# Three edits to an eight-stage decoder kernel: loads moved into the first stage, norms and output of the state space re-timed, local layers entered group by group

## The chip, the cores and the metric

The kernel runs on one core of a Trainium2 chip, as one program. The metric is the device time of the whole program in microseconds (us). Engines are named as the profile names them: PE (TensorE), DVE (VectorE), ACT (ScalarE), POOL (GpSimd) and SP (SyncE, which only issues DMAs here). All arithmetic is in float32, apart from one split into bf16 parts in the state space.

## The reference

A residual stream x of 16 sequences, 256 positions and 128 channels passes eight stages, each fed by a LayerNorm without gain or bias.

```python
x = x + causal_linear_attention(ln(x))   # "favor": 16 heads of 64, 128 random features
x = x + router_ffn(ln(x))                # "router"
x = x + cosine_attention(ln(x))          # "cosine"
x = x + int4_linear(ln(x))               # "int4"
x = x + state_space(ln(x))               # "mamba": inner 256, 16 states, silu gate
x = x + expert_ffn(ln(x))                # "experts": 8 experts, top 2
x = x + gated_recurrence(ln(x))          # "hgrn"
y = ln(x)                                # "local": 6 layers on y
for i in range(6):
    y = y + local_attention(shift_tokens(y), window=32) @ Wo[i]
    y = y + (a * gelu(gate)) @ W2[i] + b2[i]   # a, gate from an affine LayerNorm of the shifted y
return x + y
```

`shift_tokens` delays the upper half of the channels by one position. In the state space, for each of 256 inner channels and 16 states, h = exp(delta·A)·h + delta·x·B runs along the sequence, and C reads it out.

## The kernel before

**Tiles and groups.** x stays in SBUF as 32 tiles of 128 positions. Four tiles make a group of 512 columns (`GT` = 4, `GROUPS` = 8). Each stage is written as one loop of steps, and in a step each engine has its own list of helper calls, in an order set by hand. Engines meet only at semaphores: an instruction list is run in order, so a wait holds back all that stands behind it on its engine. Between blocks (`nc.Block()`) all engines meet.

**First block** (`build`, L2852 to L2866). SP issues group 0 of x, nine constants, the favor weights, the rest of x, and then 38 loads for the stages router, cosine, int4, mamba and hgrn (`Weights.load`, L2744). Then it waits for the constants. The other engines have nothing to do in it.

**First stage** (`favor_attention`). 64 pairs of heads, one a step; step i projects pair i. In a step SP runs `send_inverse(i - 5)`, 4 DMAs, and `send_norm(i - 1)`, 8 DMAs, which spread small rows over the partitions. DVE's `lower(n)` waits for the norms of pair n, `normalize(n)` for its inverse. At step 0, DVE's list begins with `measure(1)`, the statistics of group 1, and it waits there for x's second load; the copy of the first projection (`take`, L423) stands behind it.

**State space** (`state_space`). A step k is one state of one group: 16 steps a group, 128 in all. DVE: `drive_with(k)` (L1432), then other work that is due, then `scans(k)` (L1442). PE: `spread_rows(k)` (L1247 and L1250), `gather(k - 2)` (L1258), then work that is due. `drive_with(k)` needs `spread_rows(k)`, and that the drive before it is done. Work of the next group and of the last one is due at fixed places of the 16:

```python
MEASURE, NORMALIZE, TURN, TURNED, WIDEN, LOWER, BIAS, LOWER_C, BIAS_C, LAST_DT, SPLIT_ALL, SOFTPLUS, DELTA = \
    0, 1, 2, 3, 5, 7, 8, 9, 10, 11, 12, 13, 14
GATE, WAY_OUT, ADD_OUT = 2, 3, 4
```

The first gather of a group (at place 2) waits until DVE has read the sums of the group before (`skip_and_gate`, place 2). `project_out` (24 products) is all at place 3 on PE. `widen` (place 5) alternates with ACT's `silu`, and its second product waits for `add_out` of two groups before, since both use bank 1.

**Local layers** (`local_layers`). A block of its own comes first: SP issues 8 constants, 2 rows of scales and 11 weights; DVE takes statistics of all 32 tiles (L2190, L2193), then normalizes group after group (L2202), PE turns each group (L2230), and ACT and DVE copy the two halves into y (L2223, L2207). DVE then takes the peaks of the scales. The main block has 32 steps a layer, four quads of heads for each group, and step i runs four projections `project(4i)` to `project(4i + 3)`. Each goes round a ring: PE projects into the one bank (L2254), DVE multiplies it twice (`rotate_start`, L2539 and L2540), ACT squares it (`square`, L2433), and PE's next projection waits for that square. POOL sums squares and multiplies by the inverse norms (L2645, L2653), which come by 4 DMAs a step. PE's output projection of a group is in two parts at step 4G + 6. At a layer's start DVE makes eight tables ahead of its first rotation (`scale_tables`, L2527 and L2528). Bank 7 (`X_BANK`) is used in turns; `take_x` waits until the user before has been read.

## Time and profile before

| | |
|---|---|
| time, median of 3 runs | 6522.08 us (6519.73 to 6525.92) |
| time of the profiled execution | 6522.74 us |
| its span | 6520.8 us |
| busy: PE, DVE, ACT, POOL | 90%, 67%, 52%, 35% |
| mean granted PE clock | 0.947 |
| first stage | 38 to about 900 us |
| scan of the state space | 1819 to about 2475 us |
| local layers, with the block ahead | 3201 to 6520 us |

A timeline row gives start, duration, engine, line, operation, names and count, and in brackets how long the engine had been idle and what ended that. SPq rows are DMA issues on SP. A window row gives the stretch and its length, then the busy time and count of PE, PEld, DVE, ACT and POOL, the granted clock of PE (1.00 is 2.4 GHz, 0.50 is 1.2 GHz) and the load of the DMA engines.

### The profile page before, as it was taken

Reading aid. Unit: us, or ns where it says so; the run is one execution under the profiler, and the core shown is the slowest. Engines: PE = TensorE matmul, PEld = TensorE weight load, DVE = VectorE, ACT = ScalarE, POOL = GpSimd, SP = SyncE. Lnnn points to the kernel's source line nnn. Section 1 sums busy time; section 2 is a strip of 40 time slices with the busy share of each in tenths; the row PEclk is TensorE's granted clock in tenths of the full one; section 3 lists DMA queues with packets and bytes.
Section 4 is the critical chain, followed back from the end, with each engine's and each line's share of the span. In section 5 each row is a group of like instructions: output and inputs, shape, how many; then the busy total and the mean of one; then the engine's idle time right before and its main releaser. Section 6 shows DMA issues by size and latency. Waiting matters only on the chain.

```text
span 6520.8 us, 129965 instructions
## 1 busy us (share of the span) xinstructions
PE 5878.9 (90%) x51681; PEld 3219.8 (49%) x51681; DVE 4384.8 (67%) x7178; ACT 3402.6 (52%) x5560; POOL 2289.2 (35%) x1597
## 2 busy tenths in 40 slices
PE   7999878999677778998689999999999999999998
PEld 3555554444422225765445555555555555555554
DVE  4656434454288894334678888888878788887885
ACT  3444324656144443444456656666666666665664
POOL 0111101222034441000055555555555555555553
PEclk9999978999688888998799999999999999999998
DMA  5555302333100000000011111111111111111110
GB/s 138 115 115 119 89 0 53 80 82 83 44 3 0 0 0 1 1 0 1 24 36 32 40 43 34 31 47 37 34 45 38 33 44 40 34 39 41 38 37 24
DMA packets 298945, 275.95 MB, mean 42 GB/s; under 512 B 40580, under 2 KB 289572, under 8 KB 298148
## 3 DMA queue, kind: packets, MB, share of 16 engines
q1 hardware_dynamic: 298372, 268.00, 17.7%
q8 instruction: 397, 6.50, 0.4%
q14 instruction: 176, 1.44, 0.1%
HBM read 30.88 MB, written 2.10 MB: 5 GB/s over the span
## 4 chain that ended last, share of the span: by engine, by line
PE 33%; issue 5%; DVE 5%; POOL 5%; ACT 2%; DMA 0%; POOLq 0%; DVEq 0%; SPq 0%; ACTq 0%
PE banks L2254 7%; PE banks L2289 6%; PE banks L2324 5%; PE banks L2309 4%; PE banks L2267 3%; PE banks L2341 3%; DVE local_probs L2559 2%; POOL local_rot L2653 2%; POOL local_ssum L2645 2%; PE banks L2363 2%; PE banks L2313 2%; PE banks L2274 1%; ACT local_probs L2455 1%; DVE local_gate L2584 1%; DVE local_sin L2540 1%
## 5 line engine op out<-in xcount | busy, mean ns | idle before, releaser
L2645 POOL TENSOR_TENSOR local_ssum<-local_sq 128x512 f32<-128x512 f32 x384 | 697.5, 1816 | 2145.1 <-ACT local_sq L2433 2144.6
L2653 POOL TENSOR_TENSOR local_rot<-local_rot,local_inv_all 128x512 f32<-128x512 f32 x768 | 964.6, 1288 | 94.1 <-DMA local_inv_all<-local_inv 93.6
L2254 PE MATMUL banks<-local_y,local_Wqkv 128*128 128x512 f32 x1536 | 823.0, 618 | 64.0 <-ACT local_sq L2433 61.2
L2559 DVE TENSOR_TENSOR local_probs<-banks,band 128x576 f32<-128x576 f32 x768 | 546.2, 753 | 185.4 <-PE banks L2289 180.1
L2455 ACT ACTIVATE local_probs<-local_probs,local_npeak 128x1152 f32<-128x1152 f32 x384 | 482.8, 1257 | 357.1 <-DVE local_probs L2559 357.1
L2539 DVE TENSOR_TENSOR local_rot<-banks,local_rotary_scaled 128x512 f32<-128x512 f32 x768 | 525.6, 684 | 191.1 <-PE banks L2254 185.6
L2433 ACT ACTIVATE local_sq<-banks 128x512 f32<-128x512 f32 x768 | 459.4, 598 | 253.6 <-DVE local_sin L2540 244.8
L2546 DVE TENSOR_TENSOR local_rot<-local_rot,local_sin 128x1024 f32<-128x1024 f32 x384 | 513.7, 1338 | 41.9 <-DVE local_sin L2540 2.3
L2449 ACT COPY local_v<-banks 128x512 f32<-128x512 f32 x384 | 224.9, 586 | 594.1 <-PE banks L2267 593.6
L2289 PEld LDWEIGHTS banks<-local_rot 32*128 32x128 f32 x12288 | 416.7, 186 | 225.0 <-issue 200.8
L2540 DVE TENSOR_TENSOR local_sin<-banks,local_rotary_scaled 128x512 f32<-128x512 f32 x768 | 522.4, 680 | 0.0
L2309 PEld LDWEIGHTS banks<-local_probs,local_v 128*32 128x32 f32 x12288 | 345.4, 110 | 301.8 <-issue 291.9
L2289 PE MATMUL banks<-local_rot 32*128 32x160 f32 (+1 forms) x12288 | 490.2, 296 | 0.0
L1361 POOL TENSOR_TENSOR mamba_seen<-mamba_state,mamba_c_wide 128x1024 f32<-128x1024 f32 x128 | 301.0, 2352 | 474.2 <-DVE mamba_state L1442 474.2
L2309 PE MATMUL banks<-local_probs,local_v 128*32 128x160 f32 (+1 forms) x12288 | 458.5, 290 | 0.5 <-DVE local_oT L2567 0.5
L2254 PEld LDWEIGHTS banks<-local_y,local_Wqkv 128*128 128x128 f32 x1536 | 264.3, 190 | 372.1 <-ACT local_sq L2433 249.5
L1031 POOL TENSOR_TENSOR cosine_summed<-cosine_probs 128x512 f32<-128x512 f32 x128 | 162.4, 1269 | 696.1 <-ACT cosine_probs L919 696.1
L2267 PE MATMUL banks<-local_Wqkv,local_y 128*128 128x512 f32 x768 | 396.0, 597 | 0.0
L2324 PE MATMUL banks<-local_oT,local_Wo 128*128 128x512 f32 x768 | 354.9, 605 | 0.9 <-ACT local_gate L2477 0.9
L1258 PE MATMUL banks<-mamba_seen,ident 128*128 128x512 f32 x512 | 289.2, 693 | 64.8 <-DVE mamba_xs L1449 42.3
L2341 PE MATMUL banks<-local_mlp_z,local_W 128*128 128x512 f32 (+1 forms) x576 | 328.2, 652 | 11.9 <-DVE local_gate L2584 4.2
L487 POOL TENSOR_TENSOR favor_summed<-favor_probs 128x256 f32<-128x256 f32 x128 | 93.0, 727 | 689.3 <-DVE favor_probs L443 689.3
(400 smaller groups left out, 10561.4 us busy)
## 6 DMA issues: line engine op xcount, KB each, us to landing
local_inv_all<-local_inv SPq DMA_DIRECT2D x768, 128.0 KB, 2.7
favor_half_norm_all<-favor_half_norm SPq DMA_DIRECT2D x512, 128.0 KB, 3.0
cosine_inv_all<-cosine_inv SPq DMA_DIRECT2D x256, 128.0 KB, 2.6
favor_rden<-favor_inv SPq DMA_DIRECT2D x256, 64.0 KB, 2.1
cosine_rden<-cosine_inv_den SPq DMA_DIRECT2D x256, 64.0 KB, 2.1
local_Wqkv<-in_L_ffn_Wqkv_quads SPq DMA_DIRECT2D x36, 256.0 KB, 2.9
local_Wo<-in_L_ffn_Wo_quads SPq DMA_DIRECT2D x6, 512.0 KB, 4.1
experts_w_W<-in_L_ffn_W SPq DMA_DIRECT2D x1, 2048.0 KB
```

Of the source, the lines that this page charges most:

```text
L2254: pe.matmul(seqs(banks[:, QK_BANK, :]), Wqkv[:, at:at + P], y_group(g), start=True, stop=True).then_inc(qk_projected, 1)
L2267: pe.matmul(banks[:, V_BANK, :], y[:, 2 * g + tile // ST, at:at + P], Wqkv[:, V_COLUMNS(half)], start=True, stop=True).then_inc(v_projecte ...
L2289: last = pe.matmul(banks[:, S_BANK + r, lo:hi], k[rows_r, half, at:at + P], q[rows_r, half, at:at + hi - lo], start=(half == 0), stop=(hal ...
L2309: last = pe.matmul(banks[rows_r, O_BANK, part * SEQ + at:part * SEQ + to], v[:, G % 2, s * ST + tile, c:c + 32], probs[:, e % 3, r, lo:hi] ...
L2324: last = pe.matmul(banks[:, X_BANK, :], Wo[:, j, :], oT[:, (QUADS * G + j // 2) % (QUADS + 1), j % 2, :], start=(j == 0), stop=(j == 2 * Q ...
L2341: pe.matmul(banks[0:m, X_BANK, :], W1[:, column + lo:column + lo + m], z[:], start=True, stop=True).then_inc(signal, 1)
L2455: act.activation(a, a, ACT.Exp, bias=npeak[:, layer:layer + 1], scale=SCALE).then_inc(exped, 1)
L2539: dve.tensor_tensor(seqs(rot[:, k % ROTATED, half, :]), raw, twice(table[:, m, 0, half, :]), ALU.mult).then_inc(cosined, 1)
L2540: dve.tensor_tensor(seqs(sin[:, m, half, :]), raw, twice(table[:, m, 1, half, :]), ALU.mult).then_inc(sined, 1)
L2559: dve.tensor_tensor(probs[:, e % 3, r:r + 2, :], banks[:, S_BANK + r:S_BANK + r + 2, 0:SCORES], consts["band"].unsqueeze(1).broadcast_to([ ...
L2645: pool.tensor_tensor(ssum[:, n % 2, m, :], sq[:, 0, :], sq[:, 1, :], ALU.add).then_inc(square_summed, 1)
L2653: pool.tensor_tensor(a, a, twice(inv_all[:, n % 2, m, of_seq(s)]), ALU.mult).then_inc(united, 1)
```

## The change

**One, loads.** The first block keeps group 0 of x, four constants, the favor weights and the rest of x. The other five constants are issued by SP within the first stage, at step 1, and the loads of router, cosine, int4, mamba and hgrn at steps 2 to 6, each time behind that step's `send_norm`. The order among the loads is kept. At the end of its list for the stage SP waits for all constants.

**Two, state space.** The norm of the next group is due four places earlier (places −4 to −1, that is 12 to 15 of the group before), the loop starts four steps earlier, PE's turn waits in addition until bank 0 is free, `project_out` is halved over places 3 and 4, and `add_out` is at place 5.

**Three, local layers.** The block ahead norms, turns and copies group 0 alone; ACT now copies both halves. Group i + 1 is measured, rooted and normalized in step i, and turned and copied in step i + 1, for i = 0 to 6, through bank 7 and a tile of 512 columns. The four tables of q are made at the end of the step before a layer starts, the four of k behind the first rotation.

```diff
# favor_attention, SP
+                    if i == LOADS:
+                        for tile, source in w["later_consts"]:
+                            sp.dma_start(tile, source).then_inc(w["consts_loaded"][0], 16)
+                    if 0 < i - LOADS <= len(w["later"]):
+                        w["later"][i - LOADS - 1].load(sp)
+                sp.wait_ge(*w["consts_loaded"])
...
# state_space
-        0, 1, 2, 3, 5, 7, 8, 9, 10, 11, 12, 13, 14
-    GATE, WAY_OUT, ADD_OUT = 2, 3, 4
-    FIRST, LAST = -NS, N + ADD_OUT
+        -4, -3, -2, -1, 5, 7, 8, 9, 10, 11, 12, 13, 14
+    GATE, WAY_OUT, ADD_OUT = 2, (3, 4), 5
+    FIRST, LAST = MEASURE - NS, N + ADD_OUT
...
                 def turn(m):
                     pe.wait_ge(normed, GT * (m + 1))
+                    if m:
+                        pe.wait_ge(dt_biased, CH * m)
...
-                def project_out(g):
+                def project_out(g, half):
                     pe.wait_ge(gated, CH * (g + 1))
-                    for t in range(GT):
+                    for t in range(half * GT // 2, (half + 1) * GT // 2):
...
-                    if (g := finish_at(k, WAY_OUT)) is not None:
-                        project_out(g)
+                    for half in range(2):
+                        if (g := finish_at(k, WAY_OUT[half])) is not None:
+                            project_out(g, half)
...
# local_layers, helpers of the entry
+        def measure(dve, g):
+            for tile in tiles_of(g):
+                dve.bn_stats(ln_stats[:, tile, :], x[:, tile, :]).then_inc(stats_done, 1)
+            for tile in tiles_of(g):
+                dve.wait_ge(stats_done, tile + 1)
+                dve.bn_aggr(ln_moments[:, tile, :], ln_stats[:, tile, :]).then_inc(moments_done, 1)
...
+        def normalize_x(dve, g):
+            dve.wait_ge(rstd_ready, g + 1)
+            if g:
+                dve.wait_ge(turned, g)
...
+        def turn_x(pe, g):
+            pe.wait_ge(normed, GT * (g + 1))
+            for tile in range(GT):
+                last = pe.transpose(banks[:, X_BANK, tile * P:(tile + 1) * P], xn[:, tile, :], consts["ident"])
+            last.then_inc(turned, 1)
+
+        def copy_x(act, g):
+            act.wait_ge(turned, g + 1)
+            for side, a in y_sides(g):
+                act.copy(a, seqs(banks[side, X_BANK, :])).then_inc(y_ready, 1)
...
# PE, in project(c), and in a step behind score(odd)
+                        if layer == 0 and quad == 0:
+                            pe.wait_ge(y_ready, 2 * (g + 1))
...
+                    if 1 <= i < GROUPS:
+                        take_x(y_ready, 2 * (i + 1))
+                        turn_x(pe, i)
...
# ACT, behind exp(odd) and ahead of square(4i + 3)
+                    if 1 <= i < GROUPS:
+                        copy_x(act, i)
+                    if i < GROUPS - 1:
+                        root_x(act, i + 1)
...
# DVE
                     if i < N:
+                        if i == 0:
+                            scale_tables(0, 0)
+                        rotate_start(4 * i)
                         if i % STEPS == 0:
-                            scale_tables(i // STEPS)
-                        rotate_start(4 * i)
+                            scale_tables(i // STEPS, 1)
...
                         rotate_start(4 * i + 1)
                         rotate_end(2 * i)
+                        if i % STEPS == STEPS - 1 and i < N - 1:
+                            scale_tables(i // STEPS + 1, 0)
+                    if i < GROUPS - 1:
+                        measure(dve, i + 1)
...
                         rotate_start(4 * i + 3)
                         rotate_end(2 * i + 1)
+                    if i < GROUPS - 1:
+                        normalize_x(dve, i + 1)
...
# build
+FAVOR_CONSTS = ("ident", "ones", "heads_of_pair", "causal")
-                for n in consts:
+                for n in FAVOR_CONSTS:
                     sp.dma_start(consts[n], t[n]).then_inc(consts_loaded, 16)
                 ws["favor"].load(sp)
                 sp.dma_start(x[:, GT:TILES, :], rows[:, GT:TILES, :]).then_inc(x_rest, 16)
-                for name in ("router", "cosine", "int4", "mamba", "hgrn"):
-                    ws[name].load(sp)
-                sp.wait_ge(consts_loaded, 16 * len(consts))
+                sp.wait_ge(consts_loaded, 16 * len(FAVOR_CONSTS))
```

## Rows read from the trace of the kernel before

**Rows 1.** Timeline, first 60 us: start, duration, engine, line, operation, count [idle before].
```profile
9.12 1.14 SPq L2860 DMA_DIRECT2D x<-in_L_attn_x  x1
10.30 8.39 SPq L2744 DMA_DIRECT2D router_w_W1T<-in_L_ffn_W1T  x1
...
37.42 0.43 SPq L2744 DMA_DIRECT2D hgrn_w_norm_w<-in_L_attn_norm_w  x1
...
45.38 0.69 DVE L423 COPY favor_qk<-banks 128x512 f32<-128x512 f32 x1 [2.76 <-PE banks L240]
```

**Rows 2.** DMA issues: count, KB each (misread where uneven), median us to landing.
```profile
local_rot<-in_L_ffn_k_scale SPq DMA_DIRECT2D x1, 192.0 KB, 5.6
...
x<-in_L_attn_x SPq DMA_DIRECT2D x1, 0.5 KB, 13.3
```

**Rows 3.** Timeline of SP's queue alone in the first stage, steps 1 to 6.
```profile
55.34 28.42 SPq L194 DMA_DIRECT2D favor_half_norm_all<-favor_half_norm  x32
87.86 2.48 SPq L205 DMA_DIRECT2D favor_rden<-favor_inv  x4
90.45 5.22 SPq L194 DMA_DIRECT2D favor_half_norm_all<-favor_half_norm  x8
98.36 2.47 SPq L205 DMA_DIRECT2D favor_rden<-favor_inv  x4
```

**Rows 4.** Timeline of the state space, second group's last steps and the join behind.
```profile
1903.17 2.10 DVE L1382 TENSOR_SCALAR mamba_xn<-x,mamba_moments,mamba_rstd 128x128 f32<-128x128 f32 x4
...
1910.23 3.60 PE L1258 MATMUL banks<-mamba_seen,ident 128*128 128x512 f32 x4 [6.31 <-DVE mamba_xs L1449]
...
1914.60 1.23 DVE L1432 TENSOR_TENSOR banks<-mamba_dx,banks 128x1024 f32<-128x1024 f32 x1 [1.07 <-PE banks L1247]
...
1915.86 2.33 DVE L1442 TENSOR_TENSOR_SCAN mamba_state<-mamba_decay,banks 128x512 f32<-128x512 f32 x2
1916.26 0.61 PE L1266 MATMUL banks<-mamba_w_Wout,mamba_xs 128*128 128x128 f32 x4
...
1920.88 1.23 DVE L1432 TENSOR_TENSOR banks<-mamba_dx,banks 128x1024 f32<-128x1024 f32 x1 [2.68 <-PE banks L1247]
...
1924.69 1.88 PE L1212 MATMUL banks<-mamba_xnT,mamba_w_Win 128*128 128x512 f32 x4
1924.97 1.23 DVE L1432 TENSOR_TENSOR banks<-mamba_dx,banks 128x1024 f32<-128x1024 f32 x1
...
1930.14 1.23 DVE L1432 TENSOR_TENSOR banks<-mamba_dx,banks 128x1024 f32<-128x1024 f32 x1 [1.57 <-PE banks L1247]
```

**Rows 5.** Timeline of the entry to the local layers.
```profile
3201.52 6.29 DVE L2190 BATCH_NORM_STATS2 local_mlp_z<-x 128x6 f32<-128x128 f32 x32 [4.53 <-PEq L46]
...
3206.68 0.55 SPq L2176 DMA_DIRECT2D local_rot<-in_L_ffn_k_scale  x1
...
3213.79 0.37 SPq L2160 DMA_DIRECT2D local_W<-in_L_ffn_W  x1
...
3232.06 1.11 DVE L2202 TENSOR_SCALAR local_rot<-x,local_mlp_sq,local_mlp_yc 128x128 f32<-128x128 f32 x4
...
3236.59 2.04 PE L2254 MATMUL banks<-local_y,local_Wqkv 128*128 128x512 f32 x2 [2.24 <-PEq L2168]
```

**Rows 6.** Windows (PE, PEld, DVE, ACT, POOL busy, PEclk, DMA) of layer steps; timeline.
```profile
3236.60:3254.60 18.00, 11.67 (x12) 3.31 (x12) 9.10 (x18) 3.36 (x6) 1.75 (x1) 0.50 0.00 0
...
3285.80:3299.50 13.70, 12.34 (x180) 7.01 (x181) 11.85 (x18) 8.35 (x15) 7.72 (x6) 1.00 0.19 41
...
3297.66 1.26 ACT L2455 ACTIVATE local_probs<-local_probs,local_npeak 128x1152 f32<-128x1152 f32 x1 [1.40 <-DVE local_probs L2559]
...
3344.23 0.69 DVE L2539 TENSOR_TENSOR local_rot<-banks,local_rotary_scaled 128x512 f32<-128x512 f32 x1 [3.04 <-PE banks L2254]
```

**Rows 7.** Timeline of VectorE where the second layer starts.
```profile
3767.05 0.34 DVE L2527 TENSOR_SCALAR local_rotary_scaled<-local_rotary,local_qk_scales 128x256 f32<-128x256 f32 x1
...
3776.78 1.53 DVE L2592 SCALAR_TENSOR_TENSOR local_y<-banks,local_b,local_y 64x512 f32<-64x512 f32 x2 [0.92 <-PE banks L2363]
```

More of the change, by code:

```diff
@@ L142, in favor_attention @@
     OUTS = 11
+    LOADS = 1
     A_BANK, F_BANK, S_BANK, O_BANK, DEN_BANK, X_BANK = 0, 1, 3, 5, 6, 7
@@ L2188, in _ @@
             def _(dve):
[L2189 to L2195 removed]
+                measure(dve, 0)
                 dve.memset(up_half[:], 16.0 * float(np.log(2.0))).then_inc(started, 1)
@@ L2199, in _ @@
                 dve.memset(y[high, :, 0:1], 0.0).then_inc(started, 1)
[L2200 to L2207 removed]
+                normalize_x(dve, 0)
                 dve.wait_ge(rows_in, 32)
@@ L2216, in _ @@
                 act.preload_act_table_set(EXP_LN)
[L2217 to L2223 removed]
+                root_x(act, 0)
+                copy_x(act, 0)
             @block.tensor
             def _(pe):
[L2227 to L2231 removed]
+                turn_x(pe, 0)
         with nc.Block() as block:
@@ L2534, in rotate_start @@
                     k = 2 * n + m
+                    if n % STEPS == 0 and half == 0:
+                        dve.wait_ge(tabled, 8 * layer_of(n) + 4 * m + 4)
                     dve.wait_ge(qk_projected, c + 1)
```

81 lines of the change are left out of this document (38 added, 43 removed).

## Prediction

> **What bounds the kernel now.** I read the page first. TensorE is busy for most of the span, but that is an average over eight stages, so each edit is priced in its own stage, from the timeline: which wait ends last there. Four places matter.
>
> The start: no engine works on data before the first block ends, and that block ends when SP has issued its last load, at 37.85 us [rows 1]. Most of these loads are not wanted before hundreds of us later.
>
> The first stage in its steady state repeats every 10.5 us, and SP issues 2.48 us of DMAs for the inverse and 5.22 us for the norms in it [rows 3]: 7.7 us of 10.5, so SP has 2.8 us to spare per step.
>
> The state space: a step of VectorE is the drive, 1.23 us, and two scans, 2.33 together, 3.63 with the gaps between them; at the join of two groups it also waits for TensorE's row spreads (L1247) [rows 4]. These waits are all that a reordering there can win.
>
> The entry of the local layers: TensorE's first projection starts at 3236.59, and the block ahead of it is VectorE's walk over all 32 tiles from 3201.52 on; SP's last issue there is over at 3214.16 [rows 5]. In the steps behind it VectorE is busy for 11.85 of 13.7 us [rows 6], so work put there is not free.
>
> **Part one, the loads.** Five constants leave the first block: 0.43 us for an issue like the last one in the rows and 0.05 to the next, 2.4 us [rows 1]. All loads from `router_w_W1T` to `hgrn_w_norm_w` leave too: from 10.30 to 37.85, 27.55 us. The block would end at 7.9. But VectorE comes to `measure(1)` before the first copy of a projection, and that waits for the rest of x. Its load was issued 1.18 us before `W1T`, at 9.12, and took 13.3 us to land [rows 2]: 22.4, in the new order 2.4 us earlier, 20.0. `measure(1)` is four tiles of statistics at 0.2 us [rows 5] and by my estimate 0.6 of aggregations and sum: 1.4. The copy behind it started at 45.38, because it waited for TensorE, which it won't by then. So the copy starts at 20.0 + 1.4 + 0.1 = 21.5 in place of 45.38: **23.9 us won**, and not the 30 us by which the block is shorter. The favor weights are issued ahead of x's rest and hide behind it, as does the first projection.
>
> The price is paid in the first stage's steps 1 to 6. The moved issues cost SP 27.55 less the 7.96 us by which `W1T`'s own 8.39 exceeds its neighbours' 0.43 [rows 1], 19.6 for 38 loads, and 2.4 for the constants: 22.0 us. On SP they stand behind `send_norm` and in front of the next step's `send_inverse` and `send_norm`; VectorE's `lower` and `normalize` wait for those. From 55.34, SP would have six norms (31.3), two inverses (5.0) and the loads (22.0) to issue before the third inverse: free at 113.6 where it is wanted at 87.86 + 21 = 108.86 [rows 3]. That is **4.8 us late, which I take as lost**. Low end 2 (a norm that lands ahead of its use absorbs the rest). A gain is excluded, since nothing is taken off SP there. High end: each of the five groups of loads stalls as `W1T` did, 8 us apiece, 45 us; what made `W1T` slow, 1.8 MB of x just issued, has an equal only in the cosine group, so 13 is my practical high end. The new wait for the constants at the end of SP's program ends long before. Net of part one: 19.1.
>
> **Part two, the state space.** VectorE's work per group is the same wherever the norm stands, so only TensorE's order counts. At the join of two groups: the gather after the skip connection starts at 1910.23 and takes 3.6 us, the next spread comes behind the four transposes, and VectorE idles 1.07 until 1914.60; then the whole projection out, from 1916.26, makes it idle 2.68 until 1920.88; widening starts at 1924.69 and makes it idle 1.57 more [rows 4]. Between the gather's end and VectorE's start lie 0.8 us, by my estimate half of it the transposes: without them the first wait is 0.6. Between 1916.26 and 1920.88 lie 4.6 us, 0.5 of it the spread up to VectorE's start, so the projection is 4.1. With halves of 2.05 us each, TensorE needs 0.5 (spreads, to VectorE's start) + 1.6 (gather, 1914.60 to 1916.26) + 2.05 = 4.15 a step against VectorE's 3.63: two waits of 0.5 in place of 2.68. The third step gets no `add_out`, so it takes 4.15 as against 4.09 before. But TensorE now comes to the widening without its lead: 1.7 us after VectorE's step start, where it was 0.28 us before it, so that step grows by 1.95 us. Sum from 1913.53 to 1930.14: before 16.6, after 0.6 + 4.15 + 4.15 + 7.1 = 16.0: 0.6 us for a group. If the gather runs at the upper clock (1.7 us in place of 3.6, since VectorE reaches the skip 1.9 us sooner, the norm of 2.10 having moved) TensorE regains its lead and it is 2.0. Seven joins: 4 to 14 us. I take **5**, near the low end, because nothing in the rows shows the clock kept over a gap of 4.4 us. The low bound below that is −4, if the longer way to the widening also delays ScalarE's next decays at every join. The extra steps ahead of the first hold no work of their own.
>
> **Part three, the local layers.** The block ahead now holds one group: norm, four transposes and copies are over by 3209. The peaks wait for the `k_scale` load, 3206.68 + 5.6 [rows 2, 5], plus the 1.2 us of reduction: 3213.5. SP's last issue ends at 3214.16 and sets the end; the first projection starts at 3214.5 in place of 3236.59: **22.1 won**.
>
> The other seven groups now run inside steps 0 to 7. On VectorE each costs `measure`, 0.2 us a tile for the statistics [rows 5] and, with aggregations and sum, 1.4 as in part one, and a normalization, 1.11 with GpSimd idle [rows 5] or 2.10 with it busy [rows 4]; GpSimd works in most of these steps, so 3.5 together for the pair at most and 2.5 at least. On ScalarE: two copies and two roots, by my estimate 1.6, put between `exp` and the `square` that releases the next projection. In steps 2 to 5 `exp` (3297.66 + 1.26) ends just when `square` is due [rows 6], so these 1.6 and VectorE's normalization are both late, side by side: 1.7. `measure` costs 1.4 less the 0.5 of VectorE's wait for the scores: 0.9. So 2.6 a step, 10.4 for four. Step 0 has wide waits because TensorE runs at the low clock there: 0.6. Step 1: 1.9. In step 6 VectorE waits 3.04 us for TensorE's output projection [rows 6], which hides its part; ScalarE's and the transposes' leave about 0.5 each in steps 6 and 7. **14 us paid**, 8.1 net.
>
> Here the Trainium skill speaks against the change: SBUF — State Buffer, section "Who interferes with whom", says that VectorE's scalar-tensor operations can take a port pair that they share with GpSimd, whole and for the full instruction. By that rule the seven normalizations cost 2.1 each, by the rows of the idle prologue 1.11; the payment would be 16 or 12. The row beside a busy GpSimd (2.10) agrees with the rule.
>
> The tables at a layer's start are eight operations of 0.26 us apart, all ahead of the first rotation [rows 7]. Split four and four they free that rotation by 1.05 us; VectorE has no gap there until 3776.78, where it waits 0.92 for TensorE [rows 7]. Between 0 and 0.9 at each of five layers: **1.5**.
>
> **Sum**: 19.1 + 5 + 8.1 + 1.5 = 33.7. The profiled execution took 6522.7 (its span is 6520.8), 0.7 above the median: 6522.1 − 33.7 = 6488, say **6489**.
>
> **The rivals.**
> - SP becomes the first stage's bound: every group of loads stalls its queue. For it: SP is at 73% there and `W1T` once took 8.39 us. Against: the groups are a step apart. 13 to 45 us in place of 4.8: 6497 to 6529, most likely 6505.
> - The new work in the layers is hidden. For it: the chain of waits in steps 1 to 6 runs through GpSimd and the transfer of the norms rather than VectorE. Paid 3 in place of 14: 6478.
> - It adds up instead, VectorE's 3.5, ScalarE's 1.6 and TensorE's 0.5 in series, 5 us in seven steps: 35 paid, 6510.
> - The change doesn't do what it says at the joins: TensorE is late for the widening in any order, no gain in part two: 6494.
> - Slower: TensorE's clock. Step 0 runs at a granted 0.5, the lower level of 1.2 GHz, and takes 18.0 us; step 3 at 1.00 (2.4 GHz) takes 13.7 [rows 6]: 4.3 us a step. If the waits that the by-group work puts into the first steps keep TensorE at the lower level, they give back the whole gain and the 13 us beside it after 11 steps; with 16, 6489 + 69 = 6558. Against: the level rose within two steps, in spite of wide gaps.
>
> **How the numbers follow.** Forecast 0.50 (6481 to 6497), SP bound 0.12, hidden 0.16, in series 0.11, no gain at the joins 0.07, clock 0.04. The range 6474 to 6505 takes in the hidden case and the bounds of parts one and two, and leaves out most of the series case, the clock and SP's upper half. 0.2% is 13 us, about what a measurement of this kernel can tell from no change. Only the clock ends beyond it: slower 0.04; half of SP's and of the series case end within it: same 0.10; faster 0.86.
>
> **What would show it.** First copy of `favor_qk` near 21.5; the spacing of `favor_rden`'s issues above 10.5 us for three or four steps, then back; at a join of the state space VectorE's waits for the row spreads near 0.6, 0.5 and 0.5, and a longer one in the widening step; the first layer projection 22 us after the first layer load less 9, that is 13 us after it in place of 35; steps 2 to 5 of the layers at 16 to 17 us. The prediction is wrong if x's rest lands much later than 20, or if steps 1 to 7 grow by over 5 us each.

## The result, and the profile after

| | before | after |
|---|---|---|
| median of the timed runs | 6522.08 us (6519.73 to 6533.43, 5 runs) | 6484.81 us (6481.32 to 6486.44, 5 runs) |
| ratio to before, 95% interval | | 0.9943 [0.9933, 0.9954] |
| profiled execution, its span | 6520.8 us | 6482.8 us |
| mean granted clock | 0.947 | 0.950 |

The forecast was 6489. Timed again beside e9 (below), the changed kernel had 6476.88 us and a ratio of 0.9926 [0.9913, 0.9940]. The two intervals overlap, and the kernel's own median moved by 8 us between them: a few microseconds can't be read from medians, so the parts are followed in the traces, by the start of the same instruction in each.

The ledger of the two profiled executions, in us that the changed kernel is ahead of the one before. It comes from starts of VectorE's instructions. (In the kernel before the last `favor_oT` starts at 798.0 us and the stage is over at 811, not near 900.)

```
first copy of favor_qk                 25.3   (20.06 against 45.38)
end of the first stage (last favor_oT) 17.6
state-space stage, first statistics    17.3
first drive of the scan                15.2
last drive of the scan                 26.1
local block, first rotation            48.9
local layers, head of step 9           34.8
last rotation of the last layer        37.3
span                                   38.0
```

**The start.** VectorE's timeline. The columns are start, duration, engine, line, operation, tiles, count and [idle before and what ended it].

```profile
18.80 0.87 DVE L409 BATCH_NORM_STATS2 favor_stats<-x 128x6 f32<-128x128 f32 x4 [7.38 <-DMA x<-in_L_attn_x]
...
20.06 0.69 DVE L430 COPY favor_qk<-banks 128x512 f32<-128x512 f32 x1
```

The first row ends its wait with the landing of x's rest, issued at 6.87 and so 11.9 us on its way; the copy answers to the one at 45.38 [rows 1].

**SP's queue in the first stage** (the send of the inverses, L206), with one group of loads in front of the third, and VectorE's two waits for what they carry:

```profile
65.94 2.49 SPq L206 DMA_DIRECT2D favor_rden<-favor_inv  x4
...
80.33 2.49 SPq L206 DMA_DIRECT2D favor_rden<-favor_inv  x4
...
88.13 0.61 SPq L2786 DMA_DIRECT2D hgrn_w_Wq<-in_L_attn_Wq  x1
...
92.58 3.67 SPq L206 DMA_DIRECT2D favor_rden<-favor_inv  x4
...
101.73 2.48 SPq L206 DMA_DIRECT2D favor_rden<-favor_inv  x4
...
84.35 0.69 DVE L457 TENSOR_TENSOR favor_oT<-banks,favor_rden 128x512 f32<-128x512 f32 x1 [2.76 <-DMA favor_rden<-favor_inv]
...
97.79 0.69 DVE L457 TENSOR_TENSOR favor_oT<-banks,favor_rden 128x512 f32<-128x512 f32 x1 [3.86 <-DMA favor_rden<-favor_inv]
```

Before, these sends were 10.5 us apart [rows 3]. Here the distances are 14.4, 12.3 and 9.2, and VectorE stands 2.76 and 3.86 us.

**The join of two state-space groups**, the same one as in [rows 4]: VectorE's drives with their waits.

```profile
1895.77 1.23 DVE L1442 TENSOR_TENSOR banks<-mamba_dx,banks 128x1024 f32<-128x1024 f32 x1 [0.99 <-PE banks L1256]
...
1900.23 1.23 DVE L1442 TENSOR_TENSOR banks<-mamba_dx,banks 128x1024 f32<-128x1024 f32 x1 [0.87 <-PE banks L1256]
...
1904.40 1.23 DVE L1442 TENSOR_TENSOR banks<-mamba_dx,banks 128x1024 f32<-128x1024 f32 x1 [0.57 <-PE banks L1256]
...
1911.51 1.23 DVE L1442 TENSOR_TENSOR banks<-mamba_dx,banks 128x1024 f32<-128x1024 f32 x1 [3.05 <-PE banks L1256]
```

The waits were 1.07, 2.68, none and 1.57 before; they are 0.99, 0.87, 0.57 and 3.05. Their sum is no smaller: 5.3 before, 5.5 after.

**The entry of the layers.** TensorE's first projection (before at 3236.59 [rows 5]), then step 6: TensorE's output projection, ScalarE's exponential and copy ahead of it, and VectorE's first rotation of the next step.

```profile
3187.76 2.04 PE L2280 MATMUL banks<-local_y,local_Wqkv 128*128 128x512 f32 x2 [9.45 <-PEq L2214]
...
3300.91 1.25 ACT L2484 ACTIVATE local_probs<-local_probs,local_npeak 128x1152 f32<-128x1152 f32 x1 [0.73 <-DVE local_probs L2592]
3302.07 1.17 ACT L2212 COPY local_y<-banks 64x512 f32<-64x512 f32 x2
...
3303.34 6.61 PE L2350 MATMUL banks<-local_oT,local_Wo 128*128 128x512 f32 x8 [3.72 <-issue]
...
3310.84 0.69 DVE L2572 TENSOR_TENSOR local_rot<-banks,local_rotary_scaled 128x512 f32<-128x512 f32 x1 [9.97 <-PE banks L2280]
```

The copy L2212 is what empties bank 7, and the projection out takes this bank: it starts 0.1 us behind the copy's end, after 3.72 us of idleness, and its eight products take 6.61 us. VectorE stands 9.97 us, where it stood 3.04 before in this place [rows 6].

Windows of step 0 and step 3 (columns: window, length, busy us of PE, PEld, DVE, ACT and POOL, granted clock, DMA share, GB/s); before, they were 18.0 and 13.7 us long [rows 6]:

```profile
3187.70:3205.00 17.30, 10.87 (x13) 3.49 (x14) 10.63 (x27) 3.66 (x8) 2.06 (x2) 0.60 0.24 70
3239.00:3256.00 17.00, 14.34 (x187) 8.11 (x188) 15.97 (x30) 10.58 (x20) 9.19 (x7) 1.00 0.15 32
```

Step 3 has VectorE busy for 15.97 of 17.0 us, where it was busy for 11.85 of 13.7, and TensorE's clock is 1.00 in both: VectorE's 4.1 us of added work are enough for the 3.3 by which it is longer.

### The profile page after: what moved, and what is told of

It reads as the page before. It is cut to its first block, busy times and chain, and to the rows that moved or that the text cites. A ratio compares the mean times of both kernels' runs of the same rounds, so it can differ in the third digit from the quotient of the medians.

```text
span 6482.8 us, 130017 instructions
## 1 busy us (share of the span) xinstructions
PE 5881.0 (91%) x51681; PEld 3217.2 (50%) x51681; DVE 4381.4 (68%) x7177; ACT 3410.3 (53%) x5582; POOL 2283.7 (35%) x1597
## 3 DMA queue, kind: packets, MB, share of 16 engines
q1 hardware_dynamic: 298372, 268.00, 17.8%
## 4 chain that ended last, share of the span: by engine, by line
PE 31%; issue 8%; POOL 7%; DVE 3%; ACT 2%; POOLq 0%; DMA 0%; SPq 0%; DVEq 0%; ACTq 0%
PE banks L2280 7%; PE banks L2315 5%; PE banks L2350 4%; PE banks L2335 4%; POOL local_rot L2694 4%; PE banks L2293 3%; POOL local_ssum L2686 3%; PE banks L2367 3%; PE banks L2389 2%; PE banks L2339 2%; DVE local_probs L2592 2%; PE banks L2300 1%; ACT local_probs L2484 1%; ACT local_sq L2462 0%; PE banks L2363 0%
## 5 line engine op out<-in xcount | busy, mean ns | idle before, releaser
L2686 POOL TENSOR_TENSOR local_ssum<-local_sq 128x512 f32<-128x512 f32 x384 | 683.1, 1779 | 2137.0 <-ACT local_sq L2462 2136.6
L2579 DVE TENSOR_TENSOR local_rot<-local_rot,local_sin 128x1024 f32<-128x1024 f32 x384 | 499.7, 1301 | 40.8 <-DVE local_sin L2573 0.9
L2367 PE MATMUL banks<-local_mlp_z,local_W 128*128 128x512 f32 (+1 forms) x576 | 329.1, 654 | 19.6 <-DVE local_gate L2617 11.9
```

The costliest lines, as they stand in the source:

```text
L2367: pe.matmul(banks[0:m, X_BANK, :], W1[:, column + lo:column + lo + m], z[:], start=True, stop=True).then_inc(signal, 1)
L2686: pool.tensor_tensor(ssum[:, n % 2, m, :], sq[:, 0, :], sq[:, 1, :], ALU.add).then_inc(square_summed, 1)
```

## The experiments

Each kernel is compared with the kernel before by its time, and by its trace with whatever it stands beside.

### One part alone: e1, e2, e3

e1 has only part one's edits of the diff above, e2 only part two's, e3 only part three's.

> The kernel before with part one alone: only the loads needed by the first stage are issued at entry, those of the later stages within its steps. Theory (the parts act apart and add up; the changed kernel's trace has the first stage's last product 17.6 us earlier, and 17.3 at the state-space stage's start): 17.5 us shorter, about 6504.5, with the first x copy near 20 and the sends of favor_rden at spacings of about 14.4, 12.3, 9.2, 10.5 us. Rival (the later stages and the start of the local layers depended on the order of loads, so part of the gain seen in the whole belongs to the other parts or is eaten at a later stage's first load): 10 us or less, over 6512.

> The kernel before with part two alone: in the state-space stage the norm of the next group moved to before the seam of two groups, and the output product in two halves. Theory A (the work taken off the seams is all of it, the gain seen over that stage in the whole kernel, 10.3 us, is its own): about 6511.8, with the scan's period per group lower in the groups whose gather after the seam runs at the upper clock. Theory B (the forecast's sum of 5 us was right for the part itself and the rest of the 10.3 is a drift of the clock that came with the changed start): about 6517.

> The kernel before with part three alone: the local layers entered by groups and their tables split. Theory A (entry gains 21.1 us, the layers' first eight steps give back 14.1 and the rest wins about 3, as the whole kernel's trace shows): 10 us shorter, about 6512, with the stall of TensorE ahead of project_out at step 6 near 3.7 us and that step near 26.8 us. Theory B (the loss at step 6 is chance in the phase of the first steps and comes from the shifted start): step 6 back at about 20.3 us, and 16 us shorter, about 6506.

| | median, us | ratio to before | span | lead at the first stage's end | won in the state space | won at the entry | won in layer steps 0 to 8 | lead at the last rotation |
|---|---|---|---|---|---|---|---|---|
| before | 6519.16 | | 6520.8 | | | | | |
| e1 | 6498.56 | 0.9967 [0.9955, 0.9979] | 6499.8 | 18.7 | 0.0 | 0.0 | 1.6 | 20.8 |
| e2 | 6506.94 | 0.9979 [0.9970, 0.9989] | 6515.1 | −1.8 | 10.7 | 0.0 | 0.3 | 1.6 |
| e3 | 6503.65 | 0.9980 [0.9971, 0.9989] | 6495.3 | 1.0 | 1.4 | 24.9 | −12.6 | 23.3 |

(The spans and leads are against the first profiled execution of the kernel before; minus is a loss. The entry is counted from the recurrent stage's first statistics to the first rotation of the layers.) The product of the three ratios is 0.9926, and the changed kernel has 0.9943 and 0.9926: **the parts add up, as closely as these ratios can tell.** The single traces are coarser. Their spans are 21.0, 5.7 and 25.5 us ahead, 52 together, where the two traces of the changed kernel have 38.0 and 39.8. For these 12 to 14 us no cause is shown; lines that these edits don't touch move by several us (e2 and e3 win 4.1 and 2.1 us behind the last rotation, e3 another 2.1 in the recurrent stage and 1.4 in the state space).

In the traces each part gains where it stands. e1 is 16.7 to 23.1 us ahead from the first stage's end on. e2 wins 10.7 us in the state space against 10.3 in the whole, so by the stage theory A holds for it and B falls. e3 loses its 12.6 us in steps 0 to 8, and TensorE's wait at step 6 is 3.72 us there too and the step 25.5 us long: that isn't chance from the shifted start. By its time e3 is nearer to theory B (6506 expected there, 6512 by A, 6503.65 measured), but it is the step that tells the two apart. Its entry gives 24.9 us by this table, but 2.1 of them were won within the recurrent stage that stands in the same interval and isn't edited; without them it is 22.8, and the traces with all three parts have 21.2 to 22.9. e2 also shows the noise: it loses 4.3 us in stages that it shares line by line with the kernel before, 1.8 of them in the first, where its TensorE rose to the upper level later (the sixth projection, at 57.50, took 1.12 us before; the same one and the next take 2.07 and 2.08 in e2).

### What the state space gains from: e7, e8, e11

e7 moves the norms alone, e8 only halves the output product:

```diff
 # e7, on before
-        0, 1, 2, 3, 5, 7, 8, 9, 10, 11, 12, 13, 14
+        -4, -3, -2, -1, 5, 7, 8, 9, 10, 11, 12, 13, 14
-    FIRST, LAST = -NS, N + ADD_OUT
+    FIRST, LAST = MEASURE - NS, N + ADD_OUT
...
                 def turn(m):
                     pe.wait_ge(normed, GT * (m + 1))
+                    if m:
+                        pe.wait_ge(dt_biased, CH * m)
 # e8, on before
-    GATE, WAY_OUT, ADD_OUT = 2, 3, 4
+    GATE, WAY_OUT, ADD_OUT = 2, (3, 4), 5
...
```

> The kernel before with only the state space's norms moved ahead of the seam of two groups, the output product whole. Theory A (VectorE's statistics and normalization lay on the seam and were most of it): the scan's period falls by 0.8 to 1.2 us in each of the groups 1 to 6, 5 to 7 us of the stage's 10.3. Theory B (the output product in front of the gather and the row spreads was most of it): 2 us or less.

> The kernel before with only the state space's output product in two halves in two steps, the norms where they were. Theory A (the norms are most of it): 2 to 4 us over the stage. Theory B (the output product in front of the gather and the row spreads, and the clock that falls in the gap before it, were most of it): 5 us or more, and with e7 the two parts add up to about 10 us.

e7: 6510.43 us, ratio 0.9987 [0.9977, 0.9996]. e8: 6514.95 us, 0.9994 [0.9985, 1.0004], which is no difference that can be measured. The traces separate them: over the stage, up to the first statistics of the next one, e7 wins 7.8 us and e8 3.0, together 10.8 against e2's 10.7. For e7 that is theory A, a little above its 5 to 7 us and not in the way it said: it wins 0.8 us or more only in three of groups 1 to 6. For e8 it is theory A too (2 to 4 us). Durations of the scan's steps, from one drive's start to the next, in group 5 of 0 to 7, and the periods:

```
step of group 5      0     1     2     3     4     5    12     13
before             4.93  5.52  7.82  6.31  4.10  5.16  10.52  3.63
e7 norms           3.63  3.63  6.97  7.10  4.10  5.17  11.46  5.51
e8 halves          4.92  5.52  7.83  4.29  4.17  7.11  10.52  3.63
after              3.63  3.63  6.96  5.08  4.16  7.11  11.46  5.53

period of group      0      1      2      3      4      5      6    last 15 steps   all
before             77.55  84.46  84.89  85.11  85.22  85.27  85.48    61.20       649.18
e7 norms           77.16  83.70  85.04  83.44  84.38  84.85  80.56    60.58       639.71
e8 halves          77.52  84.37  84.83  85.07  85.22  85.26  85.49    59.72       647.48
after              77.16  84.23  84.82  83.34  84.32  84.83  80.55    59.01       638.26
```

The norm leaves steps 0 and 1 (1.30 + 1.89 us) and is paid in steps 12 and 13 (0.94 + 1.90): 0.35 us won by the move. What e7 wins is mostly elsewhere: group 6 had the norm of group 7 in its steps and now has none, 4.9 us in one period (3.2 of them in steps 0 and 1, 1.4 in step 2). The norm of group 1 went ahead of the scan, which costs 2.1 us there (lead 17.3 at the stage's head, 15.2 at the first drive). The halves move 2.0 us from step 3 to step 5 and win nothing in the scan, save in the last group, where no widening follows, 1.5 us. Behind the last drive, the way to the last `add_out` takes 16.3 to 16.5 us in the nine kernels with halves and 17.4 to 17.8 in the four without, so there they win some 1.3 more.

The step that holds the late gather (step 2) takes 7.05 to 7.82 us in groups 1 to 6 before and 6.0 to 6.97 in e7. TensorE's rows show two reasons. The next group's four transposes stood between the gather and the row spreads (0.27 us each in group 1, 0.42 in the later groups) and no longer do. And TensorE stands idle for 4.0 to 4.4 us ahead of the gather in place of 6.3, and its clock rises sooner: the gather takes 3.60 to 3.75 us before and 2.8 to 3.8 in e7. The last 15 steps take 0.6 us less in e7; e3, which doesn't edit this stage, has the same 60.58, so that isn't won by the move.

e11 cuts the moved norm's work and keeps its instructions:

```diff
-                        dve.bn_stats(stats[:, t, :], tiles(m)[:, t, :])
+                        dve.bn_stats(stats[:, t, :], tiles(m)[:, t, 0:D if m < 2 else 8])
+                        n = D if m < 2 else 1
-                        dve.tensor_scalar(xn[:, t, :], tiles(m)[:, t, :], moments ...
+                        dve.tensor_scalar(xn[:, t, 0:n], tiles(m)[:, t, 0:n], moments ...
```

> The changed kernel, with the work of the state space's norms cut: for the groups 2 to 7 the statistics are taken over 8 of 128 elements and one element is normalized, so these groups' results are not the reference's; instructions, waits and signals stay. Theory A (VectorE sets the scan's pace in the norm's new place as in the old, so the norm's time is still paid there: steps 12 and 13 of a group take 11.46 and 5.53 us with it, 10.52 and 3.63 in the last group but one, which has none): these steps fall to 10.5 to 10.8 and 3.7 to 4.2 us, and each of five periods shortens by 2 to 2.7 us. Theory B (the norm is hidden there, and the longer steps come from the waits and signals that it adds): they stay within 0.3 us of 11.46 and 5.53.

Steps 12 and 13 took 11.24 and 4.22 us. Step 13 fell by 1.30 us and decides for A; step 12 fell by 0.22 only, which taken alone B would allow. The rows say why: the normalization of group 2 and GpSimd's product beside it, in the changed kernel, then in e11.

```profile
1950.68 2.12 DVE L1392 TENSOR_SCALAR mamba_xn<-x,mamba_moments,mamba_rstd 128x128 f32<-128x128 f32 x4
1949.58 2.35 POOL L1371 TENSOR_TENSOR mamba_seen<-mamba_state,mamba_c_wide 128x1024 f32<-128x1024 f32 x1 [9.11 <-DVE mamba_state L1452]
```

```profile
1946.28 0.81 DVE L1393 TENSOR_SCALAR mamba_xn<-x,mamba_moments,mamba_rstd 128x1 f32<-128x1 f32 x4
1945.19 2.35 POOL L1371 TENSOR_TENSOR mamba_seen<-mamba_state,mamba_c_wide 128x1024 f32<-128x1024 f32 x1 [8.89 <-DVE mamba_state L1453]
```

The cut takes 2.12 − 0.81 = 1.31 us from it, and the step shortens by 1.30: **every microsecond of the norm is on the path in its new place.** But only 0.3 of the 1.3 us are the arithmetic that was cut. The first of the four whole normalizations takes 1.35 us and ends at 1952.02, 0.08 behind the end of GpSimd's product, the other three take 0.34 each; of one element, all four take 0.27 while the same product runs. So half of the norm's 2.12 us was this meeting with GpSimd. The kernel before had it in the old place as well (1.34 us for the first, from 1987.63). In step 12 the four statistics take 0.5 us less, but the variance behind them, an operation on 128x4, now takes 0.47 us in place of 0.17 and ends 0.02 behind GpSimd's product, which leaves the 0.22.

Six periods fell by 1.4 to 2.9 us, the norm's 1.5 and what steps 2 and 3 gained. e11 was timed once, at 6463.2 us.

### Step 6 of the layers: e4

e4 is the changed kernel with two lines of ScalarE's program exchanged:

```diff
+                    if 1 <= i < GROUPS:
+                        copy_x(act, i)
                     if (e := within(2 * (i - 2) + 1)) is not None:
                         exp(e)
-                    if 1 <= i < GROUPS:
-                        copy_x(act, i)
```

> The changed kernel, but ScalarE copies the turned x of the next group ahead of the odd exponential in the first steps of the local layers, not behind it. Theory A (in steps 1 to 7 bank 7 is held by this copy, which stands behind an exponential that waits for a mask; at step 6 TensorE stood 3.72 us ahead of project_out for it, and its clock then fell and the eight products took 6.61 us in place of 3.7): the copy is done 1.2 to 2 us sooner, the wait of TensorE at step 6 falls to 2.5 us or less, the products take near 3.7 us, step 6 shortens by 3 to 6 us, and the whole by about as much: 6479 to 6482. Theory B (something else holds TensorE there, the mask or the projection): step 6 stays near 26.8 us, 6485 within 1.

6474.80 us, ratio 0.9930 [0.9917, 0.9944]; by the intervals that can't be told from the changed kernel. In its trace ScalarE's copy, the exponential and TensorE's products of step 6:

```profile
3299.99 1.17 ACT L2212 COPY local_y<-banks 64x512 f32<-64x512 f32 x2
3301.18 1.25 ACT L2484 ACTIVATE local_probs<-local_probs,local_npeak 128x1152 f32<-128x1152 f32 x1
...
3301.26 3.67 PE L2350 MATMUL banks<-local_oT,local_Wo 128*128 128x512 f32 x8 [1.73 <-issue]
...
3305.83 0.69 DVE L2572 TENSOR_TENSOR local_rot<-banks,local_rotary_scaled 128x512 f32<-128x512 f32 x1 [5.04 <-PE banks L2280]
```

The windows of step 6, first of the changed kernel, then of e4:

```profile
3288.80:3315.60 26.80, 21.56 (x199) 11.11 (x198) 16.40 (x35) 9.91 (x18) 9.03 (x7) 0.87 0.09 21
```

```profile
3288.60:3310.60 22.00, 17.74 (x197) 9.88 (x197) 16.53 (x34) 9.80 (x18) 9.39 (x7) 1.00 0.11 26
```

Theory A holds with the numbers it gave: the wait is 1.73 in place of 3.72, the products take 3.67 in place of 6.61, and the step 21.84 in place of 26.76; the time is below the 6479 to 6482 expected. Of the 4.9 us only 2.0 are the copy's own; 2.9 are the clock, which in these two traces stayed at its upper level behind the shorter wait and fell behind the longer one (mean 1.00 and 0.87 of these windows). The other traces bear out the 2.0 and not the 2.9. The four kernels with the copy behind the exponential all wait 3.72 us: products 6.61 us and step 26.76 in the changed kernel, 5.4 and 25.5 in e3, e10 and e11. The four with the copy ahead all wait 1.73: 3.67 and 21.8 in e4, e5 and e9, but in e6 the clock fell behind the same wait, and the step took 23.5:

```profile
3297.28 5.37 PE L2350 MATMUL banks<-local_oT,local_Wo 128*128 128x512 f32 x8 [1.73 <-issue]
```

The lead was there at step 8 (38.6 against 32.8) and gone at the last rotation (37.6 against 37.3): the boundaries of layers took 4.3 us of it, which e6 is about.

### The first stage's queue: e5

On e4, with one load for each step, from the sixth step on (`moves` is the list of all moved loads):

```diff
-    LOADS = 1
+    LOADS = 5
-                    if i == LOADS:
-                        for tile, source in w["later_consts"]: ...
-                    if 0 < i - LOADS <= len(w["later"]):
-                        w["later"][i - LOADS - 1].load(sp)
...
+                    if 0 <= i - LOADS < len(moves):
+                        tile, source, loaded = moves[i - LOADS]
+                        sp.dma_start(tile, source).then_inc(loaded, 16)
```

> The kernel of e4, but the later stages' loads are issued one for each step of the first stage from its sixth step on, not five to twelve in each of five steps from the second on. Theory A (SP's backlog is what ate 7.7 of the 25.3 us won at the start: the sends of favor_rden were 14.4, 12.3, 9.2 and 10.5 us apart in place of 10.5 each, and VectorE waited 2.76 and 3.86 us for them): the sends come at 10.5 us again, the waits for favor_rden go, and the first stage ends 22 to 25 us before the kernel before in place of 16.7; 6470 or a little less. Theory B (the loss comes from the granted clock, which stays lower in the first steps when they start 25 us earlier, not from the loads): the first stage's end stays at 17 to 19 us sooner.

6468.75 us, ratio 0.9918 [0.9905, 0.9932]. SP's queue:

```profile
62.46 2.49 SPq L206 DMA_DIRECT2D favor_rden<-favor_inv  x4
...
70.28 0.60 SPq L218 DMA_DIRECT2D band<-in_band  x1
...
72.96 2.48 SPq L206 DMA_DIRECT2D favor_rden<-favor_inv  x4
...
83.46 2.48 SPq L206 DMA_DIRECT2D favor_rden<-favor_inv  x4
```

The sends are 10.5 us apart, VectorE no longer waits for `favor_rden`, and the first stage ends 25.4 us ahead: all that was won at its start, against 16.7 in e4. Theory A. The clock is the same in the two: the projection that starts near 32 us is the first at the upper level in e4 and e5 (1.13 and 1.12 us). In the changed kernel that one and the next, at 35.03, took 2.07 and 2.08; the rise came later, as in e2. ScalarE had its first inverse ready at 65.45, where it was 64.37 in e10 with the early rise and the same loads, and 62.44 in e5. So the late rise is worth some 1 us there, and it cost next to nothing, since SP was behind anyway (the stage's end is 17.6 us ahead in the changed kernel, 18.0 in e10).

### The tables: e6

On e4, with the first four table products back at the layer's head:

```diff
-                        if i == 0:
-                            scale_tables(0, 0)
+                        if i % STEPS == 0:
+                            scale_tables(i // STEPS, 0)
                         rotate_start(4 * i)
-                        if i % STEPS == STEPS - 1 and i < N - 1:
-                            scale_tables(i // STEPS + 1, 0)
```

What led to it is the changed kernel's trace at the boundary of the third and fourth layer, GpSimd and VectorE in order of time:

```profile
4782.33 1.75 POOL L2686 TENSOR_TENSOR local_ssum<-local_sq 128x512 f32<-128x512 f32 x1 [8.33 <-ACT local_sq L2462]
4782.87 1.36 DVE L2559 TENSOR_SCALAR local_rotary_scaled<-local_rotary,local_qk_scales 128x256 f32<-128x256 f32 x1
4784.15 0.34 DVE L2560 TENSOR_SCALAR local_rotary_scaled<-local_rotary,local_qk_scales 128x256 f32<-128x256 f32 x1
4784.34 5.06 POOL L2694 TENSOR_TENSOR local_rot<-local_rot,local_inv_all 128x512 f32<-128x512 f32 x4 [0.26 <-DMA local_inv_all<-local_inv]
4784.41 1.36 DVE L2559 TENSOR_SCALAR local_rotary_scaled<-local_rotary,local_qk_scales 128x256 f32<-128x256 f32 x1
4785.69 1.35 DVE L2560 TENSOR_SCALAR local_rotary_scaled<-local_rotary,local_qk_scales 128x256 f32<-128x256 f32 x1
...
4788.35 1.12 PE L2367 MATMUL banks<-local_mlp_z,local_W 128*128 128x512 f32 x2 [2.75 <-DVE local_gate L2617]
...
4791.76 2.15 PE L2335 MATMUL banks<-local_probs,local_v 128*32 128x160 f32 x32
```

A table product takes 0.34 us [rows 7]. Here the first one starts while GpSimd works on `local_ssum` (until 4784.08) and ends at 4784.23, 0.15 us behind it. The third and fourth meet the instructions of `unite`, four of 1.27 us each, and end with the first and second of them. VectorE is 3.1 us late, TensorE waits 2.75, and its next products over the probabilities take 2.15 where they take 1.19 in steady steps. This agrees with the Trainium skill, SBUF — State Buffer, section "Who interferes with whom": a tensor-scalar operation of VectorE can want a port pair that it shares with GpSimd, and then, in its words, "the other **fully blocks** (not throttle)".

> The kernel of e4, but the first four table products of the next local layer stand at the head of its first step again, not in the last step of the layer before; the other four stay behind the first rotation. Theory A (a table product that meets a running instruction of GpSimd ends only with it: in the last step of a layer the first of the four took 1.36 us in all of five layers, and in the layers where the third and fourth took 1.36 too, that step took 19.1 to 20.3 us in place of 16.5, TensorE waiting 2.75 us): all table products take 0.34 us, the two steps around each boundary take 32 to 33 us together, none 35 or more, and the layers end about 8 to 10 us sooner than in e4; about 6465. Theory B (the long steps are falls of the granted clock that come with or without the table products): steps of 19 to 20 us stay in two or three of five boundaries and nothing is won.

6465.36 us (6462.69 to 6465.98), ratio 0.9916 [0.9903, 0.9930]. The last step of a layer and the first of the next together, in us, from first rotation to first rotation, with the number of table products above 1 us in brackets:

```
layers        1/2        2/3        3/4        4/5        5/6      sum
before     33.45 (0)  34.47 (0)  32.86 (0)  33.30 (0)  34.82 (0)  168.9
e1         35.27 (1)  34.48 (0)  32.86 (0)  33.35 (0)  33.24 (0)  169.2
e2         35.25 (0)  34.87 (0)  34.48 (0)  34.93 (0)  34.69 (0)  174.2
e7         35.25 (0)  34.75 (0)  32.86 (0)  33.24 (0)  33.23 (0)  169.3
e8         35.18 (0)  34.61 (0)  34.42 (0)  33.42 (0)  34.88 (0)  172.5
after      32.36 (1)  32.37 (1)  35.95 (3)  35.03 (3)  32.36 (1)  168.1
e3         32.37 (1)  32.37 (1)  35.06 (3)  33.38 (2)  32.37 (1)  165.6
e4         32.37 (1)  35.28 (3)  35.94 (3)  36.38 (3)  32.37 (1)  172.3
e5         32.37 (1)  36.28 (3)  35.02 (3)  37.32 (3)  32.37 (1)  173.4
e10        33.40 (2)  37.17 (3)  37.18 (3)  35.37 (3)  32.37 (1)  175.5
e11        32.37 (1)  32.37 (1)  35.97 (3)  36.49 (3)  32.37 (1)  169.6
e6         32.40 (0)  31.80 (0)  31.81 (0)  31.80 (0)  32.20 (0)  160.0
e9         32.29 (0)  32.33 (0)  31.80 (0)  31.80 (0)  32.16 (0)  160.4
```

With the split in the layer's last step the pair takes 32.4 us when one product meets GpSimd, 33.4 with two, 35.0 to 37.3 with three; which it is depends on when the transfer that `unite` waits for lands (0.89 us behind `ssum` at a good boundary, 0.26 here). Without any meeting it is 31.8 to 32.4. Theory A, with 12.3 us won against e4 at these five places; of the whole time the intervals of e4 and e6 overlap, the traces' spans are 6477.2 and 6460.7. (The pair also varies with no meeting at all: 168.9 to 174.2 in four of the kernels with all eight products at the head.)

### All three together, and the changed kernel again: e9, e10

e9 has the edits of e4, e5 and e6; e10 is the changed kernel.

> e5 and e6 in one kernel: the changed kernel with ScalarE's copy ahead of the odd exponential, one late load for each step of the first stage from the sixth on, and the first four table products at the head of each layer. If the three act on different places (first stage, step 6, the boundaries of layers), their gains add up: first stage's end 25 us before the kernel before, both boundary steps together 32 to 33 us, and about 6455 (6450 to 6460). If the gain at the start is given back by the clock in the layers, 6463 or more.

> The changed kernel once more, to be timed beside e9: 6485 within 4, some 25 to 30 us above e9 if that one's gains add up, and under 20 if they don't.

On one chip e9 took **6461.86 us** (6455.78 to 6463.74), ratio 0.9903 [0.9888, 0.9918], and e10 6476.88 (6469.94 to 6482.92), ratio 0.9926 [0.9913, 0.9940]. e9 is above the 6450 to 6460 expected, and the distance of 15 us is less than 25 to 30 and even than the 20 below which, by e10's expectation, the gains don't add up; the two intervals just overlap. The traces' spans are 6461.0 and 6480.9, 19.9 apart, of which the first stage gives 7.2 (leads 25.2 and 18.0), step 6 3.7 (21.83 against 25.53), the boundaries 15.1: 26.0. The other 6.1 are given back in pieces: 1.4 us between the first stage and the first rotation, 0.3 in steps 0 to 5, 2.8 in other steps of the layers, 1.7 behind the last rotation. For none of them is a cause settled. The three gains stand at their three places, but in the whole they are shown to add up only in part. e9 has the lowest median of this study. e6, which has the copy's edit and the tables', can't be told from it: 6465.36 us, ratios 0.9916 and 0.9903 with intervals that overlap, and spans of 6460.7 and 6461.0. That the thin loads of e5 gain in the whole time beside the other two is therefore not shown.

## Why the prediction was right, and where it was not

The time was 4 us off, by terms that were off by more, in both directions.

**Part one, 19.1 forecast, 17.6 measured at the stage's end.** The start was 25.3 in place of 23.9, because x's rest took 11.9 us to land, not 13.3. It had no `W1T` and no other load behind it: it lands 11.0 to 11.9 us after its issue in the eight kernels with the loads moved and 12.4 to 13.3 in the five without. The backlog was priced at 4.8 us at the third send; it was 9.1 (92.58 against 83.46 in e5) and 7.8 from the fourth on, which e5 gives back. (The late rise of the clock has no part in it: SP issued without a gap of over 0.6 us from the first norm on.) The mechanism and the place were right; the term was short by 4.3 us of SP's own time between the first norm (30.02) and the third inverse (92.58): 62.6 us where the sum had 58.3. The loads took 24.0 in place of 22.0, the norms 31.8 in place of 31.3, and 1.8 us of gaps between issues weren't in the sum at all. The rival in which each group stalls as `W1T` did is refuted: the longest issue of a moved load is 1.38 us.

**Part two, 5 forecast, 10.3 measured** (10.7 in e2), within its bounds of 4 to 14, but not by the sum that gave the 5. That sum had seven joins alike. At the join of [rows 4] the waits came near what was drawn, 0.99, 0.87 and 0.57 in place of 0.6, 0.5 and 0.5, with a widening step longer by 1.94 us (1.95 forecast), and that period won 0.2 us. The first six periods won 3.8 us together, 0.1 to 1.8 each, so the 0.6 for a join was about right as a mean. The forecast's better case, a gather at the upper level, came in part: it takes 2.6 to 3.75 us behind 4.4 us of idleness or less, never the 1.7. The rest, 6.5 of the 10.3, stands at the two ends, which the forecast didn't count apart: a norm moved one group ahead leaves the last but one period altogether (4.9 us), the last 15 steps win 2.2, the way behind the last drive 1.5, and 2.1 are paid ahead of the scan. e7 and e8 show that the halves gain 1.7 us in the scan and 3.0 with the way out. "The extra steps ahead of the first hold no work of their own" was false: they hold the 2.1 us. The range held because it was wide, not because the sum had these ends in it.

**Part three, entry.** 22.1 forecast, 21.2 measured (27.7 at the recurrent stage, 48.9 at the first rotation), and the first projection came 13.7 us behind the first layer load. Paid: 14 forecast for steps 0 to 7, 16.1 measured there; step 8 then gives 2.0 back, which makes 14.1. That this is the forecast's number is a coincidence. Steps 1 to 5 grew by 9.7 us, the forecast had 12.3; step 0 got 0.7 shorter. Step 6 was to hide its share but for 0.5, and grew by 6.5; step 7 grew by 0.6. The failed step is "in step 6 VectorE waits 3.04 us for TensorE's output projection, which hides its part": it looked at VectorE and ScalarE, and not at who empties the bank that this projection takes. e4 shows it for the 2.0 us of the copy; the clock's part behind it is 1.7 to 2.9 us in the four traces with that order.

**The tables, 1.5 forecast, 0.8 measured in the first trace and none over all.** The sums of the five pairs have a mean of 170.7 in the six traces with the split in the last step and of 170.8 in the five with all eight products at the head. The price of 0.26 us for an operation was taken where GpSimd was idle, and the new place has it at work. The forecast had weighed this very thing for the normalizations (2.05 to 2.07 us in most of the layers' rows, as the row beside a busy GpSimd said) and not for the tables.

**The rivals.** The one with the layers' work hidden and the one in series both fall: steps 1 to 5 paid 1.9 us each on average (0.9 to 3.6). The clock rival did not come as a level kept low (the layers' steps 2 to 5 took 17.43, 17.22, 16.04 and 16.54 us, where 16 to 17 was forecast at the upper level), but as single falls behind waits of 2.75 and 3.72 us, at some 1.5 and 2.9 us, and in e6 behind one of 1.73.

## What to carry to other kernels

When an edit moves an instruction in time, price it by the row of the same kind beside the neighbours of its new place, GpSimd's above all: 0.34 us became 1.36. When work is moved one iteration ahead, count the first and the last iteration apart, since the steady ones may gain little while one of the ends gains or pays the whole. And a small copy that empties a bank belongs in front of work that waits for something else.

## What the runs showed of the hardware

A table product of 0.34 us that meets a GpSimd instruction ends 0.15 us behind it and takes 1.36; a whole normalization that does ends 0.08 us behind (1.35 in place of 0.34), and one of a single element isn't held up (0.27 us). A wait of TensorE can cost more than itself, but its length alone doesn't say whether: eight products took 5.4 to 6.6 us behind 3.72 us of idleness in four traces, and behind 1.73 us they took 3.67 in three and 5.37 in one. The clock also moves the time of lines that no edit touched: the way from the last rotation to the end of the span took 93.3 us before, 92.6 after, 89.2 in e2 and 87.2 in e4. A group of six products (L2389) behind the same 0.93 us of idleness takes 2.82 us there or 4.6 to 5.5, by the level that it meets, in the same order of instructions. A single trace's total can't be read closer than these 6 us.
